# Routing rows in one piece: gate and token number inside the dispatched row, first group of the experts fixed and loaded one stage earlier, scatters of a group in parallel

## The chip, the core and the metric

One core of a Trainium2 chip. Five engines work side by side, each with its own instruction queue: TensorE (PE; its weight loads are listed as PEld), VectorE (DVE), ScalarE (ACT), GpSimd (POOL) and SyncE (SP), which here only issues DMAs. They are ordered by semaphores. DMAs are issued from the queues of SP and ACT, and from GpSimd where rows are addressed by an index held in memory (the indirect ones). The metric is the time of one execution on the device, in microseconds; the times before are the median of three runs.

## The reference, cut to what matters

A decoder of two layers on `x` of 32 x 128 tokens, 256 wide. The first five steps (two attentions and a quantised layer, then a gated attention with a long convolution, then a cross attention) are not touched by the change beyond what is told below. After each step comes `x = layernorm(x + step(x))`. The last step is a mixture of experts:

```python
logits = x_flat @ router_w.T                       # 4096 tokens, 8 experts
probs = softmax(logits); top_v, top_i = top_k(probs, 2); top_v /= sum(top_v)
for k in range(2):                                 # first and second choice
    pos = rank of the token within expert top_i[:, k]    # in token order
    keep = pos < C                                 # C = 1280 rows per expert and choice
    h = gelu(expert_in @ w1[expert])               # 256 -> 1024
    y = h @ w2[expert]                             # 1024 -> 256
    out += y[its row] * (top_v[:, k] * keep)
```

Each token is thus handled by two experts, and its two results, each times its gate, are added to it before the last layer norm.

## The kernel before

Seven stages run one after the other, each a block in which the five engines run their own programs. Between two stages stand a barrier, the clearing of semaphores by SyncE, and another barrier. Two stages matter, and one thing in the first.

**The first stage** (`l0_attn_heads`, L235). Beside its own work SyncE clears the DRAM table `xs` with zeros, in 32 pieces, one per tile of 128 tokens (`clear`, L373), and the small table `xm`. SyncE's queue issues in order: load an input tile, clear a piece, store a tile.

**The attention stage of the last layer** (`l1_xattn`, L1907). Tiles of 128 tokens, two tiles a group (`G = 2`), 16 groups, one walk step per tile; every engine has its list of work by lag behind the current tile `n`. Each tile has two halves `u` of eight heads:

- TensorE computes scores, VectorE takes maximum and difference (`shift`), ScalarE the exponential, VectorE sums and reciprocals (`sums`), GpSimd scales (`scale_e`, L2036), TensorE transposes (`transpose_e`, L2162), ScalarE copies, TensorE applies to the values, and the output projection follows two steps later (`multiply`, L2181).
- Four steps after its scores a group is normalised: VectorE gives mean and variance, GpSimd the root and shift (`roots`, L2042 to L2048), ScalarE writes the rows into `acc` (`normalise`, L2259), a tile buffer that holds all 32 tiles. SyncE stores them to the DRAM table `xo` (`store`, L2091).
- TensorE then transposes the rows and computes the router's logits; VectorE picks the two experts (`pick_expert`), TensorE counts ranks, VectorE turns them into a slot number per token and choice (`place_rows`, L2355 to L2373). ScalarE takes the exponential for the gate (`gate_exp`).
- Six steps behind, GpSimd dispatches a tile (`dispatch`, L2056 and L2058): for each of the two choices one indirect DMA writes the 128 rows into the table `xs` at their slots, and one writes gate and token number, two words a row, into the table `xm`. These are 4 DMAs a tile, 128 in all. GpSimd's order in an even step is: bias add for the group (`bias_x`), `scale_e` for both halves, dispatch; in an odd step: `scale_e` twice, `roots`, dispatch.
- After the last tile VectorE works out which expert and which place in `xs` each of 39 groups of 256 rows has (`map_groups`). The group with number 0 has a place that is known only then, like all others.

In `xs` each expert has a region of its own; slots that no token takes stay zero.

**The experts' stage** (`moe_experts`, L2413). For each of 39 groups `j`: SyncE loads 256 rows from `xs` (`load_x`, L2491), gates and numbers from `xm` (L2493) and the expert's 2 MB of weights (`load_w`, L2482; six buffers). TensorE runs `transposes(j)`, `up(j-1)` and `down_(j-2)` per step, 32 matmuls for each product; ScalarE applies the Gelu; VectorE multiplies the result with the gate (`gate_y`, L2585); GpSimd adds the rows to `xo` with an accumulating indirect DMA, one for each 128 rows (`add`, L2473). Each of these waits until the one before it has landed. Empty slots add to a spare tile behind the last token. When all have landed, SyncE reads the rows back (L2500), and VectorE and ScalarE do the last layer norm, whose results SyncE stores.

Of the kernel before, what the change touches and what calls it, by code (L numbers as in the profile page):

```python
# [116 lines left out]
def l0_attn(nc, x_in, wgv, bgv, wo, bo, x_out, xs, xm, xo, zero, zeroed, xo_stored):  # L117

    with ExitStack() as stack:
# [8 lines left out]
        l0_attn_heads(nc, x_in, gv, va, rn, lno, ln, ident, wo, bo, x_out, xs, xm, xo, zero, zeroed, xo_stored)  # L128
# [106 lines left out]
def l0_attn_heads(nc, x_in, gv, va, rn, lno, ln, ident, wo, bo, x_out, xs, xm, xo, zero, zeroed, xo_stored):  # L235
# [4 lines left out]
    with ExitStack() as stack:  # L240
# [54 lines left out]
        with nc.Block() as block:  # L295
# [54 lines left out]
            def _(sp):  # L350
# [16 lines left out]
                per_slot = xm.rearrange("(p n) d -> p (n d)", p=P)  # L367
                for i in range(META_PARTS):
                    part = per_slot[:, D * i:min(D * i + D, 2 * deep)]
                    sp.dma_start(part, zero[:, 0:part.shape[1]]).then_inc(zeroed, 16)  # L370
# [1539 lines left out]
def l1_xattn(nc, x_in, k_in, v_in, w, router, xs, xm, xs_zeroed, acc, meta, expert, place, dispatched, xo, xo_stored):  # L1910
# [3 lines left out]
    with ExitStack() as stack:  # L1914
# [38 lines left out]
        slot = kit.sb("slot", [P, TOPK, TILES], U32)  # L1953
        cnt, grp, end = (kit.sb(n, [P, EXPERTS]) for n in ("cnt", "grp", "end"))
# [13 lines left out]
                 "counted", "placed", "based", "mapped")  # L1968
# [5 lines left out]
         counted, placed, based, mapped) = (kit.sem(n) for n in names)  # L1974
# [22 lines left out]
        with nc.Block() as block:  # L1997
            @block.gpsimd
            def _(pool):
# [39 lines left out]
                def roots(g):  # L2039
                    item_done(pool, mv_done, g, G)  # L2040
                    slot_free(pool, normed, g, 2, G)
# [7 lines left out]

                def dispatch(n):  # L2050
                    g = n // G
                    item_done(pool, placed, g, PLACE_STEPS)
                    if n == 0:
                        pool.wait_ge(xs_zeroed, (ZERO_PARTS + META_PARTS) * 16)
# [678 lines left out]
```

## Time and profile before

| what | us |
|---|---|
| median of three runs (2752.1 to 2754.99) | 2754.79 |
| the profiled execution | 2750.7 |
| its span | 2749.0 |
| TensorE busy | 2367.3 (86%) |
| VectorE busy | 1401.6 (51%) |
| ScalarE busy | 1113.6 (41%) |
| GpSimd busy | 933.3 (34%) |
| DMA engines busy, queues of SP, of GpSimd, of ACT | 29.7%, 3.8%, 3.6% of 16 engines' span |

The shares are averages over seven stages with different limits; each stage has to be read by itself. The median of all runs is 4.1 us above the profiled one, and differences are worked out within the profiled execution. A busy share of a pipelined TensorE is not its share of peak.

How the rows further down are read: in a timeline a row has its start and its duration in us from the span's start, the engine, the line of the kernel, the operation, the tile written, the tile read, shapes, the count of merged instructions, and in brackets how long the engine had been idle before it and what ended the idle time. "issue" is idle time for which the profile shows no wait. SPq and POOLq are queues of an engine. The number behind a DMA issue is the median time from issue to landing.

### The profile page before, as it was taken

What the parts mean: (1) busy time and instruction counts of PE and PEld (TensorE: products, weight loads), DVE (VectorE), ACT (ScalarE), POOL (GpSimd) and SP (SyncE); (2) the same over time, 40 slices, a digit from 0 to 9 for tenths busy, and PEclk for the clock granted to TensorE, in tenths of its full rate; (3) what the DMA queues carried; (4) which work ended last, traced back from release to release, by engine and by line L of the source; (5) the groups of instructions that cost most, each with busy time, mean ns of one, the idle gap of its engine ahead of it and who ended that gap; (6) DMA issues with size and microseconds to landing.
All of it is one profiled execution on the core that took longest, in us unless ns stands there. A gap on an engine that the chain in (4) does not pass through costs nothing. (4 is left out here: it accounts for less than half of the span.)

```text
span 2749.0 us, 44609 instructions
## 1 busy us (share of the span) xinstructions
PE 2367.3 (86%) x17103; PEld 1815.4 (66%) x17134; DVE 1401.6 (51%) x2497; ACT 1113.6 (41%) x1898; POOL 933.3 (34%) x897
## 2 busy tenths in 40 slices
PE   9688887799995768978898869999995799999993
PEld 4466666466664546745665658887884688888883
DVE  5599898387775940003544536787776011111113
ACT  2466665356554644434333235555452111111113
POOL 2455554234443770000101024565556122222221
PEclk9799999899998889999999989999997899999997
DMA  2133324300101668552121033433431765666634
GB/s 73 53 103 117 116 98 146 108 16 24 47 16 58 211 173 205 160 182 93 31 62 46 16 133 99 106 97 97 117 88 43 291 188 180 177 184 190 191 85 134
DMA packets 227409, 313.11 MB, mean 114 GB/s; under 512 B 76672, under 2 KB 209792, under 8 KB 214016
## 3 DMA queue, kind: packets, MB, share of 16 engines
q1 hardware_dynamic: 201888, 253.82, 29.7%
q0 software_dynamic: 16352, 18.69, 3.8%
q10 hardware_dynamic: 8960, 37.75, 3.6%
q8 instruction: 138, 2.26, 0.3%
q14 instruction: 71, 0.58, 0.1%
HBM read 187.58 MB, written 122.63 MB: 113 GB/s over the span
## 5 line engine op out<-in xcount | busy, mean ns | idle before, releaser
L2548 ACT ACTIVATE me_h<-me_ps_h 128x512 f32<-128x512 f32 x156 | 93.1, 597 | 461.6 <-PE me_ps_h L2528 461.6
L2585 DVE TENSOR_SCALAR me_yo<-me_ps_y,me_mt 128x256 f32<-128x256 f32 x78 | 37.8, 484 | 473.6 <-PE me_ps_y L2537 454.8
L2528 PE MATMUL me_ps_h<-me_xt,me_w 128*128 128x256 f32 x1248 | 277.0, 380 | 0.0
L2537 PE MATMUL me_ps_y<-me_w,me_h 128*128 128x256 f32 x1248 | 275.6, 379 | 0.0
L2473 POOL DMA_INDIRECT xo<-me_yo,me_row x78 | 121.8, 1562 | 452.8 <-DVE me_yo L2585 306.9
L2537 PEld LDWEIGHTS me_ps_y<-me_w,me_h 128*128 128x128 f32 x1248 | 237.1, 190 | 32.2
L2528 PEld LDWEIGHTS me_ps_h<-me_xt,me_w 128*128 128x128 f32 x1248 | 235.1, 191 | 30.6
L327 POOL TENSOR_TENSOR l0ah_cm<-l0ah_c,l0ah_after 128x1024 f32<-128x1024 f32 x64 | 151.7, 2370 | 174.3 <-DVE l0ah_c L392 174.3
L666 POOL TENSOR_TENSOR l0x_en<-l0x_e,l0x_ri 128x1024 f32<-128x1024 f32 x64 | 120.0, 1896 | 210.7 <-DVE l0x_ri L888 210.7
L2036 POOL TENSOR_TENSOR l1x_e<-l1x_e,l1x_ri 128x1024 f32<-128x1024 f32 x64 | 121.8, 1902 | 195.6 <-DVE l1x_ri L2302 194.2
L987 PE MATMUL kv_ps<-kv_w_v,kv_ct 128*128 128x512 f32 x256 | 120.2, 609 | 24.7 <-PEq L82 15.3
L980 PE MATMUL kv_ps<-kv_ct,kv_w_k 128*128 128x256 f32 x512 | 121.3, 394 | 7.4 <-ACT kv_va L1026 4.9
L547 ACT ACTIVATE l0ah_f<-l0ah_ps_s 128x1024 f32<-128x1024 f32 x64 | 65.6, 1025 | 142.8 <-PE l0ah_ps_s L476 142.7
L2143 PE MATMUL l1x_ps_p<-l1x_xct,l1x_w_q 128*128 128x256 f32 x512 | 122.9, 384 | 0.0
L2181 PE MATMUL l1x_ps_o<-l1x_w_o,l1x_ot 128*128 128x256 f32 x512 | 118.7, 385 | 1.6 <-ACT l1x_ot L2254 1.6
L980 PEld LDWEIGHTS kv_ps<-kv_ct,kv_w_k 128*128 128x128 f32 x512 | 100.8, 199 | 28.7 <-ACT kv_va L1026 6.1
L2244 ACT ACTIVATE l1x_e<-l1x_sx 128x1024 f32<-128x1024 f32 x64 | 67.5, 1055 | 126.0 <-DVE l1x_sx L2293 126.0
L847 ACT ACTIVATE l0x_et<-l0x_ps_e 128x512 f32<-128x512 f32 x128 | 69.9, 595 | 100.5 <-PE l0x_ps_e L782 100.4
L1665 DVE TENSOR_SCALAR ma_zq<-ma_zp 128x1 f32<-128x1 f32 x1 | 0.2, 154 | 210.7 <-DMA ma_same<-in_msame 210.7
L1594 POOL TENSOR_TENSOR ma_ve<-ma_mv,ma_eps 128x4 f32<-128x4 f32 x8 | 2.9, 358 | 301.0 <-DVE ma_mv L1764 301.0
L2181 PEld LDWEIGHTS l1x_ps_o<-l1x_w_o,l1x_ot 128*128 128x128 f32 x512 | 94.7, 190 | 15.4 <-ACT l1x_ot L2254 1.9
L2299 DVE TENSOR_REDUCE l1x_rs<-l1x_e 128x8 f32<-128x1024 f32 x64 | 78.0, 1219 | 48.7 <-ACT l1x_e L2244 48.3
(381 smaller groups left out, 5303.0 us busy)
## 6 DMA issues: line engine op xcount, KB each, us to landing
me_w<-in_w SPq DMA_DIRECT2D x39, 2048.0 KB, 8.6
xs<-dec_zero SPq DMA_DIRECT2D x31, 1024.0 KB, 4.6
k<-kv_kt ACTq DMA_DIRECT2D x16, 1024.0 KB, 7.0
v<-kv_va ACTq DMA_DIRECT2D x16, 1024.0 KB, 6.1
l1x_kt<-k SPq DMA_DIRECT2D x16, 1024.0 KB, 7.3
l1x_va<-v SPq DMA_DIRECT2D x16, 1024.0 KB, 5.8
me_xg<-xs SPq DMA_DIRECT2D x39, 256.0 KB, 8.6
l0ap_x<-in_x SPq DMA_DIRECT2D x32, 128.0 KB, 2.0
```

Of the source, the lines that this page charges most:

```text
L327: pool.tensor_tensor(cm[:, n % 2, u, :, :], c[:, u, :, :], after[:, :].unsqueeze(1).to_broadcast([P, HALF, P]), ALU.add).then_inc(corr_mas ...
L666: pool.tensor_tensor(en[:, n % 2, u, :, :], e[:, n % 2, u, :, :], spread(ri[:, n % 2, u, :], P), ALU.mult).then_inc(e_scaled, 1)
L980: ins = pe.matmul(bank[:, c * self.GP:(c + 1) * self.GP], self.w_k[:, k, at], self.ct[:, g % 2, k, :], start=k == 0, stop=k == 1)
L987: ins = pe.matmul(bank[:, :], self.ct[:, g % 2, k, t * P:(t + 1) * P], self.w_v[:, k, 512 * c:512 * c + 512], start=k == 0, stop=k == 1)
L2036: pool.tensor_tensor(e[:, n % 2, u, :, :], e[:, n % 2, u, :, :], spread(ri[:, n % 2, u, :], P), ALU.mult).then_inc(e_scaled, 1)
L2143: last = pe.matmul(ps_p[i % 2][:, c * GP:(c + 1) * GP], w_q[:, k, at], xct[:, k, :], start=k == 0, stop=k == 1)
L2181: last = pe.matmul(ps_o[:, 0:2, :].rearrange("p a b -> p (a b)"), ot[:, c, :], w_o[:, c, :], start=c == 0, stop=c == C - 1)
L2299: dve.tensor_reduce(rs[:, n % 2, u, :], e[:, n % 2, u, :, :], AX.X, ALU.add).then_inc(summed, 1)
L2473: pool.indirect_dma_start(token_rows, bass.IndirectOffsetOnAxis(row[:, j % 2, q:q + 1], 0), yo[:, j % 2, q, :], None, compute_op=ALU.add). ...
L2528: last = pe.matmul(ps_h[i % HB][:, f % 2, :], w[:, j % WB, FFN * c + f * P:FFN * c + f * P + P], xt[:, j % 2, c, :], start=c == 0, stop=c ...
L2537: last = pe.matmul(ps_y[q][:, 0:D], h[:, j % 2, f, q * P:(q + 1) * P], w[:, j % WB, W2 + D * f:W2 + D * f + D], start=f == 0, stop=f == FC ...
L2548: act.activation(h[:, j % 2, 2 * i:2 * i + 2, :], ps_h[i % HB][:, :, :], ACT.Gelu).then_inc(gelued, 1)
```

## The change

- Table `xm` and tile `meta` are gone. A row of `xs` has 258 words instead of 256: the row, its gate, its token number plus one. In the attention stage a ring `row` of eight tiles (four groups) holds such rows for both choices. ScalarE writes every normalised row twice, once per choice (`normed`, `doubled`); GpSimd writes the numbers (`number_rows`), VectorE the gates. 64 indirect DMAs dispatch instead of 128. The ring's writers wait until the group four before has been dispatched and stored.
- The tile buffer `acc` is no longer needed by the attention stage and is allocated in the experts' stage.
- Every expert gets at least one group (first level -1 instead of 0), so group 0 is always the first of expert 0. Its weights are loaded in the attention stage after the last value tile, and its rows at that stage's end, when SyncE has waited for all dispatches. The experts' stage loads groups 1 to 38; one of the six weight buffers is the one filled early.
- In the experts' stage gates and numbers are read from the gathered rows, of which there are six buffers instead of four; a buffer is free when its group has been gated.
- The two accumulating DMAs of a group go out without waiting for each other; they wait for both of the group before. The spare rows are 256 instead of 128, so that no two of them meet.
- The clears of the first stage write rows of 258 words; two DMAs clear the spare rows of `xo`.

```diff
@@ l0_attn_heads
-                per_slot = xm.rearrange("(p n) d -> p (n d)", p=P)
-                for i in range(META_PARTS):
...
-                sp.dma_start(xo[TILES, :, :], zero[:, :]).then_inc(xo_stored, 16)
+                for i in range(GROUP // P):
+                    sp.dma_start(xo[TILES + i, :, :], zero[:, 0:D]).then_inc(zeroed, 16)
...
-                    sp.dma_start(part, zero[:, :].unsqueeze(1).to_broadcast([P, part.shape[1], D])).then_inc(zeroed, 16)
+                    sp.dma_start(part, zero[:, :].unsqueeze(1).to_broadcast([P, part.shape[1], ROW])).then_inc(zeroed, 16)
@@ l1_xattn
+        row = kit.sb("row", [P, ROW_SLOTS, TOPK, ROW])
+        number = kit.sb("number", [P, TILES])
+        dispatched = [kit.sem(f"dispatched{b}") for b in range(ROW_SLOTS // G)]
+        RG = ROW_SLOTS // G
...
-                pool.iota(meta[:, :, :, 1], pattern=[[0, TOPK], [P, TILES]], base=1, channel_multiplier=1,
+                pool.iota(number[:, :], pattern=[[P, TILES]], base=1, channel_multiplier=1,
...
+                pool.memset(levels[:, :, 0:1], -1.0).then_inc(cut, 1)
...
+                def number_rows(g):
+                    if g >= RG:
+                        pool.wait_ge(dispatched[g % RG], 16 * TOPK * G * (g // RG))
+                    at = G * g % ROW_SLOTS
+                    pool.tensor_copy(row[:, at:at + G, :, D + 1], number[:, G * g:G * g + G].unsqueeze(2).to_broadcast([P, G, TOPK])).then_inc(numbered, 1)
+
                 def dispatch(n):
                     g = n // G
                     item_done(pool, placed, g, PLACE_STEPS)
+                    item_done(pool, numbered, g)
+                    item_done(pool, doubled, g, G)
...
                     for k in range(TOPK):
                         pool.indirect_dma_start(xs, bass.IndirectOffsetOnAxis(slot[:, k, n:n + 1], 0),
-                                                acc[:, n, :], None).then_inc(dispatched, 16)
-                        pool.indirect_dma_start(xm, bass.IndirectOffsetOnAxis(slot[:, k, n:n + 1], 0),
-                                                meta[:, k, n, :], None).then_inc(dispatched, 16)
+                                                row[:, n % ROW_SLOTS, k, :], None).then_inc(dispatched[g % RG], 16)
...
-                     [(0, lambda n: scale_e(n, 0)), (0, lambda n: scale_e(n, 1)), (3, lambda n: roots(n // G)), (6, dispatch)])
+                     [(0, lambda n: scale_e(n, 0)), (0, lambda n: scale_e(n, 1)), (3, lambda n: roots(n // G)), (3, lambda n: number_rows(n // G)), (6, dispatch)])
...
+                    if g == NG:
+                        sp.dma_start(w_first[:, :], w12[0, :, :]).then_inc(w_loaded, 16)
                     if g >= 5:
                         store(g - 5)
+                for i in range(RG):
+                    sp.wait_ge(dispatched[i], 16 * TOPK * G * NG // RG)
+                sp.dma_start(xg[:, 0, :, :], xs[0:GROUP, :].rearrange("(q p) d -> p q d", p=P)).then_inc(xg_loaded, 16)
...
                 def normalise(g):
                     item_done(act, ln_done, g)
+                    if g >= RG:
+                        act.wait_ge(dispatched[g % RG], 16 * TOPK * G * (g // RG))
+                        act.wait_ge(xo_stored[g % RG], 16 * (g // RG))
                     for t in range(G):
-                        act.activation(acc[:, G * g + t, :], r[:, g % 2, t, :], ACT.Identity, scale=ln[:, g % 2, 0, t:t + 1],
+                        act.activation(row[:, (G * g + t) % ROW_SLOTS, 0, 0:D], r[:, g % 2, t, :], ACT.Identity, scale=ln[:, g % 2, 0, t:t + 1],
                                        bias=ln[:, g % 2, 1, t:t + 1]).then_inc(normed, 1)
+                    for t in range(G):
+                        act.activation(row[:, (G * g + t) % ROW_SLOTS, 1, 0:D], r[:, g % 2, t, :], ACT.Identity, scale=ln[:, g % 2, 0, t:t + 1],
+                                       bias=ln[:, g % 2, 1, t:t + 1]).then_inc(doubled, 1)
...
-                    then(dve.tensor_tensor(meta[:, :, n:n + G, 0], kept[:, :, :], gk[:, 3:5, :], ALU.mult))
+                    if rg >= RG:
+                        dve.wait_ge(dispatched[rg % RG], 16 * TOPK * G * (rg // RG))
+                    at = n % ROW_SLOTS
+                    then(dve.tensor_tensor(row[:, at:at + G, :, D].rearrange("p t k -> p k t"), kept[:, :, :], gk[:, 3:5, :], ALU.mult))
@@ moe_experts
+        def weights(j):
+            return w[:, j % WB - 1, :] if j % WB else w_first[:, :]
...
                 def add(j):
                     item_done(pool, row_ready, j)
+                    slot_free(pool, added, j, 1, 16 * Q)
                     for q in range(Q):
-                        n = Q * j + q
-                        item_done(pool, y_gated, n)
-                        slot_free(pool, added, n, 1, 16)
+                        item_done(pool, y_gated, Q * j + q)
...
                 def load_x(j):
-                    if j == 0:
-                        sp.wait_ge(dispatched, 16 * 2 * TOPK * TILES)
                     slot_free(sp, transposed, j, XB)
-                    slot_free(sp, y_gated, j, MB, Q)
-                    slot_free(sp, row_ready, j, MB)
+                    slot_free(sp, y_gated, j, XB, Q)
+                    slot_free(sp, row_ready, j, XB)
...
-                    sp.dma_start(mt[:, j % MB, :, :], blocks(xm)[bass.ds(b, 1), :, :, :].rearrange("b p q d -> (b p) q d")
-                                 ).then_inc(mt_loaded[j % MB], 16)
-
-                unrolled(GROUPS, [(0, load_x), (0, load_w)])
+                for j in range(1, GROUPS):
+                    load_x(j)
+                    load_w(j)
```

## Rows read from the trace of the kernel before

**Rows 1.** Busy time by stretches: start:end, length, then each engine's busy us (instructions).
```profile
1696.00:1725.00 29.00, 28.94 (x244) 24.49 (x243) 23.24 (x49) 15.90 (x29) 13.96 (x14) 1.00 0.44 101
...
2165.00:2705.00 540.00, 540.00 (x2574) 475.52 (x2573) 71.71 (x189) 89.55 (x150) 118.69 (x76) 1.00 0.57 172
```

**Rows 2.** Timeline, GpSimd, first operation of `roots`: start us, duration us, instruction.
```profile
1695.28 0.19 POOL L2042 TENSOR_TENSOR l1x_ln<-l1x_mv,l1x_eps 128x2 f32<-128x2 f32 x1
...
1724.51 0.19 POOL L2042 TENSOR_TENSOR l1x_ln<-l1x_mv,l1x_eps 128x2 f32<-128x2 f32 x1
...
2060.84 0.19 POOL L2042 TENSOR_TENSOR l1x_ln<-l1x_mv,l1x_eps 128x2 f32<-128x2 f32 x1
```

**Rows 3.** Timeline, attention stage: one group; last row from a later group.
```profile
1909.68 1.04 POOL L2056 DMA_INDIRECT xs<-moe_acc,l1x_slot  x1 [0.16 <-issue]
...
1913.61 0.20 DVE L2302 RECIPROCAL l1x_ri<-l1x_rs 128x8 f32<-128x8 f32 x1
...
1914.34 1.09 ACT L2259 ACTIVATE moe_acc<-l1x_r,l1x_ln 128x256 f32<-128x256 f32 x2
1914.55 1.27 POOL L2031 TENSOR_TENSOR l1x_xb<-l1x_x,l1x_b_all 128x512 f32<-128x512 f32 x1
...
1915.78 1.89 POOL L2036 TENSOR_TENSOR l1x_e<-l1x_e,l1x_ri 128x1024 f32<-128x1024 f32 x1
...
1916.27 1.06 ACT L2244 ACTIVATE l1x_e<-l1x_sx 128x1024 f32<-128x1024 f32 x1 [0.75 <-DVE l1x_sx L2293]
...
1917.73 1.09 PE L2162 MATMUL l1x_ps_e<-l1x_ident,l1x_e 128*128 128x128 f32 x8 [1.27 <-POOL l1x_e L2036]
...
1920.65 0.84 ACT L2237 ACTIVATE l1x_qt<-l1x_ps_p,l1x_b_q 128x256 f32<-128x256 f32 x2 [1.57 <-PE l1x_ps_p L2143]
...
2070.59 1.09 PE L2162 MATMUL l1x_ps_e<-l1x_ident,l1x_e 128*128 128x128 f32 x8 [3.20 <-POOL l1x_e L2036]
```

**Rows 4.** Timeline, end of the attention stage and start of the experts' stage.
```profile
2115.08 0.96 POOL L2058 DMA_INDIRECT xm<-moe_meta,l1x_slot  x1 [5.82 <-issue]
...
2115.88 0.17 DVE L2373 CAST l1x_slot<-l1x_sf 128x4 uint32<-128x4 f32 x1
...
2133.03 0.96 POOL L2058 DMA_INDIRECT xm<-moe_meta,l1x_slot  x1 [0.30 <-issue]
...
2138.36 0.20 POOL L111 MEMSET me_ident<- 128x128 f32 x1 [4.37 <-POOLq L82]
...
2141.15 0.35 SPq L2482 DMA_DIRECT2D me_w<-in_w  x1
...
2142.26 1.09 PE L2518 MATMUL me_ps_t<-me_ident,me_xg 128*128 128x128 f32 x4 [29.46 <-DMA me_xg<-xs]
...
2150.33 1.12 PE L2518 MATMUL me_ps_t<-me_ident,me_xg 128*128 128x128 f32 x4 [6.99 <-DMA me_xg<-xs]
...
2151.24 8.25 PE L2528 MATMUL me_ps_h<-me_xt,me_w 128*128 128x256 f32 x32
```

**Rows 5.** Timeline, end of the experts' loop.
```profile
2700.69 0.48 DVE L2585 TENSOR_SCALAR me_yo<-me_ps_y,me_mt 128x256 f32<-128x256 f32 x1 [2.90 <-PE me_ps_y L2537]
...
2702.96 1.56 POOL L2473 DMA_INDIRECT xo<-me_yo,me_row  x1 [2.88 <-DMA xo<-me_yo,me_row]
...
2707.59 0.48 DVE L2585 TENSOR_SCALAR me_yo<-me_ps_y,me_mt 128x256 f32<-128x256 f32 x1 [2.90 <-PE me_ps_y L2537]
...
2712.22 1.56 POOL L2473 DMA_INDIRECT xo<-me_yo,me_row  x1 [2.81 <-DMA xo<-me_yo,me_row]
...
2715.85 7.22 SPq L2500 DMA_DIRECT2D me_r<-xo  x8
```

**Rows 6.** DMA issues: count, KB, median us to landing; then starts of the clears.
```profile
xs<-dec_zero SPq DMA_DIRECT2D x31, 1024.0 KB, 4.6
...
xs<-moe_acc,l1x_slot POOLq DMA_INDIRECT x64, 4.6
...
L375 SPq DMA_DIRECT2D xs<-dec_zero x32: 425/436/1290, 83.6 to 471.7; - x32
```

More of the change, by code:

```diff
@@ L1907, in mega_attn, with l1_xattn @@
         kit.clear_semaphores()
-def l1_xattn(nc, x_in, k_in, v_in, w, router, xs, xm, xs_zeroed, acc, meta, expert, place, dispatched, xo, xo_stored):
+def l1_xattn(nc, x_in, k_in, v_in, w, router, w12, xs, xs_zeroed, w_first, xg, w_loaded, xg_loaded, expert, place, xo, xo_stored):
     G, W = 2, 64
@@ L1973, in l1_xattn @@
          r_loaded, preset, cut, y_transposed, xr_copied, routed, lg_copied, picked, gate_exped,
-         counted, placed, based, mapped) = (kit.sem(n) for n in names)
+         counted, placed, based, mapped, doubled, numbered) = (kit.sem(n) for n in names)
         x_loaded = [kit.sem(f"x_loaded{b}") for b in range(3)]
@@ L2090, in store @@
                     item_done(sp, normed, g, G)
-                    sp.dma_start(rows(xo, g), acc[:, G * g:G * g + G, :]).then_inc(xo_stored, 16)
+                    at = G * g % ROW_SLOTS
+                    sp.dma_start(rows(xo, g), row[:, at:at + G, 0, 0:D]).then_inc(xo_stored[g % RG], 16)
                 for g in range(2, NG + 5):
@@ L2191, in transpose_y @@
                         for k in range(2):
-                            last = pe.transpose(ps_p[1][:, (2 * t + k) * P:(2 * t + k + 1) * P], acc[:, G * rg + t, k * P:(k + 1) * P], ident[:, :])
+                            last = pe.transpose(ps_p[1][:, (2 * t + k) * P:(2 * t + k + 1) * P], row[:, (G * rg + t) % ROW_SLOTS, 0, k * P:(k + 1) * P], ident[:, :])
                     last.then_inc(y_transposed, 1)
@@ L2444, in moe_experts @@
          added, stats_done, mv_done, std_done, rstd_done, shift_done, normed, stored) = (kit.sem(n) for n in names)
-        w_loaded = [kit.sem(f"w_loaded{i}") for i in range(WB)]
-        xg_loaded = [kit.sem(f"xg_loaded{i}") for i in range(XB)]
-        mt_loaded = [kit.sem(f"mt_loaded{i}") for i in range(MB)]
+        w_loaded = [w_first_loaded] + [kit.sem(f"w_loaded{i}") for i in range(1, WB)]
+        xg_loaded = [xg_first_loaded] + [kit.sem(f"xg_loaded{i}") for i in range(1, XB)]
         r_loaded = [kit.sem(f"r_loaded{i}") for i in range(NB)]
+        def weights(j):
+            return w[:, j % WB - 1, :] if j % WB else w_first[:, :]
         def blocks(a):
@@ L2527, in up @@
                             for c in range(2):
-                                last = pe.matmul(ps_h[i % HB][:, f % 2, :], w[:, j % WB, FFN * c + f * P:FFN * c + f * P + P],
+                                last = pe.matmul(ps_h[i % HB][:, f % 2, :], weights(j)[:, FFN * c + f * P:FFN * c + f * P + P],
                                                  xt[:, j % 2, c, :], start=c == 0, stop=c == 1)
@@ L2537, in down_ @@
                             last = pe.matmul(ps_y[q][:, 0:D], h[:, j % 2, f, q * P:(q + 1) * P],
-                                             w[:, j % WB, W2 + D * f:W2 + D * f + D], start=f == 0, stop=f == FC - 1)
+                                             weights(j)[:, W2 + D * f:W2 + D * f + D], start=f == 0, stop=f == FC - 1)
                         last.then_inc(down, 1)
@@ L2676, in decoder_stages @@
     mega_attn(nc, x3, xn, mx, {k[1:]: v for k, v in t.items() if k[0] == "m"}, x4)
-    l1_tail(nc, x4, k1, v1, {k[1:]: v for k, v in t.items() if k[0] == "y"}, t["router"], t["w12"], xs, xm, xs_zeroed, xo, xo_stored, out)
+    l1_tail(nc, x4, k1, v1, {k[1:]: v for k, v in t.items() if k[0] == "y"}, t["router"], t["w12"], xs, xs_zeroed, xo, xo_stored, out)
 def kernel(**inputs):
```

70 lines of the change are left out of this document (35 added, 35 removed).

## The prediction

> **What bounds the kernel now.** I read the page's slices first, then the busy time by stretches, then the waits and the timeline of the two stages that the diff touches. The last layer's attention stage runs from 1589 to about 2138 us, the experts' stage from there to 2749. Nothing before 1589 is altered, but for the zeroing in the first stage.
>
> In the middle of the experts' stage TensorE has no gap: 540.00 us busy of 540 at full clock [rows 1]. The 2574 instructions there are 68 a group (4 transposes, 64 matmuls), so one group costs 540 / (2574 / 68) = 14.3 us; 39 groups come, and their number stays. Nothing that loads, gates or scatters during it can shorten it; gains lie at its two ends.
>
> In the attention stage TensorE is busy 28.94 us of 29 in the stretch 1696:1725 [rows 1], before GpSimd's scatters run in every step. `roots` comes once per group of two tiles, so its starts give the period: 29.23 us between 1695.28 and 1724.51, then 336.33 us over 11 groups, 30.57 each [rows 2]. So 1.34 us per group is lost once scatters run. The timeline of one group shows where: four scatters and the add of the bias stand on GpSimd between `roots` and the first `scale_e` of the next tile. VectorE has the reciprocal ready at 1913.81, GpSimd starts the scaling only at 1915.78, and TensorE's transposes of that tile wait 1.27 us for it [rows 3]. TensorE is the bound except for that wait, and the wait belongs to GpSimd's queue.
>
> **The change part by part.** All sums are against the profiled execution, 2750.7 us with a span of 2749.0; the median of the runs is 2754.79, 4.1 us (0.15%) higher, and I take differences over to it.
>
> *Half the scatters in the attention stage.* The gate and number ride in the row, so 64 of 128 scatters go. Four of them last from 1909.68 to 1914.55, 4.87 us, and with the gap between two each costs 1.27 us [rows 3]; two fewer are 2.5 us. One small copy of the token number is added behind `roots`; the nearest row is a GpSimd operation on 128x2 at 0.19 us [rows 2], and I take 0.25. The bias add then runs from about 1912.3 to 1913.6, and the scaling begins as VectorE's reciprocal ends, near 1913.9 instead of 1915.78. That is 1.9 us earlier, more than TensorE's 1.27, so the wait goes and 0.6 us of slack stays. A wider row might cost GpSimd more to issue. The dearest scatter in the trace is the accumulating one at 1.56 us against 1.04 [rows 3, 5]; with 0.5 to 0.6 more for each of the two, 1.1 us comes back and half the gain is left. I take 1.3 us x 11 groups = 14.3 us (bounds 0 and 14.7). The last group with projections over waits 3.20 us [rows 3]; of it I take 1.8 (0 to 2.3).
>
> *ScalarE writes every normalised row twice.* 32 activations more: 1.09 us a pair, 16 pairs, 17.4 us of engine time. Queued behind the second pair are the gate's exponential, the second exponential of the tile, and two bias passes of the projection. ScalarE stands idle 0.75 us before that exponential [rows 3], so it comes 0.3 us late. It then does 3.1 us of work and is free at about 1919.5, which is when TensorE, 1.27 us earlier than now, delivers the projection that is now biased at 1920.65. So the pair is just covered; without that cover it costs 1.09 us per group. In the drain of the stage, where projections have ended, one pair does lie ahead of the last output projection: -0.7 (0 to -1.1).
>
> *New waits in that stage.* ScalarE, VectorE and GpSimd now wait for a row buffer that was scattered and stored four groups before. Scatters of group g-4 are issued five tile steps, about 75 us, ahead of its reuse and land in 4.6 us [rows 6]. Cost nothing; what is queued behind the waiting instruction on each engine would be the exponentials, the placement and `scale_e`. Three new small operations in the setup have no reader for 100 us. Attention sum: 14.3 + 1.8 - 0.7 = 15.4 us.
>
> *The end of the stage.* The last slots are written at 2115.88, but GpSimd still has its backlog, with one stall of 5.82 us before 2115.08, and issues its last scatter at 2133.03; the next stage starts at 2138.36 [rows 4]. With half of them, tiles 28 and 29 are done before 2115.9, and the last four go out at 2116.3, 2117.6, 2118.9 and 2120.1. Here the change adds a wait: SyncE waits for all of them inside the stage, then issues the first gather. Landing takes 4.6 us [rows 6]: 2124.7, plus 0.5 for the issue. The way from there through the barrier is not shown alone; it is between 0 and the 4.37 us from GpSimd's last instruction to the next stage [rows 4]. I take 2.4, and 1 us for the chance that the stall moves along. Start at 2128.6 instead of 2138.4: 9.8 us (5.5 to 13).
>
> The Trainium skill (DMA: Bandwidth & Descriptors, "Anatomy of one DMA") gives about 2.0 us fixed cost for a GpSimd DMA, nearly all of it the receipt from memory. By it the landing would be 2.3 us and the gain 12.1; the trace shows 4.6, and I go by that.
>
> *First group loaded early.* Now the first gather lands by 2142.26, 3.9 us after the start. The 2 MB of weights go out at 2141.15, the second gather behind them, and TensorE gets its second transposes only at 2150.33 and the first up-projection at 2151.24, 12.88 us after the start [rows 4]. After: weights and first rows are there, the second gather stands first in the queue and lands 3.9 us after the start, and the up-projection follows 0.9 later, at 4.8. Gain 8.1 us (7 to 9). Next late are the second group's weights. They are issued about 2.3 us after the start and, like the first now, land within 9.2 (2141.15 to 2150.33), at 11.5; needed at 4.8 + 8.3 + 0.5 = 13.6. Two us of cover, none of it in the sum. The early weight load stands on SyncE behind the last value tile, when no input load is left; only stores of finished rows queue behind it.
>
> *In the middle of the experts' stage* 39 small loads go, and SyncE now waits for a gated group before it loads rows, ahead of the weights. Both are for six groups later, 85 us; nothing. The two extra words per row widen each gather by 0.8%.
>
> *Scatters in pairs.* Now each scatter waits for the one before it: 2702.96, 2712.22, rows read back at 2715.85 [rows 5]. After: the second of group 37 goes at 2701.9 (gated at 2700.69 + 0.48, plus 0.7 for the hand-over), lands 4.0 later at 2705.9; group 38's first starts 2706.6, its second needs its gated half (2707.59 + 0.48) and goes at 2708.8, landing by 2708.8 + 3.6 to 4.6. Readback at about 2712.9: 3.0 us (2 to 3.5). In the steady stretch GpSimd idles anyway.
>
> Sum: 15.4 + 9.8 + 8.1 + 3.0 = 36.3 us. 2754.8 - 36.3 = 2718.5 (the profiled one 2714.4).
>
> **The rivals.**
>
> *A. ScalarE takes GpSimd's place.* For it: the slack worked out above is nil, and the new pair is 1.09 us against a wait of 1.27. Against it: ScalarE is idle at other points of the group, and a delay of 0.2 or 0.3 leaves most of the gain. If the period stays at 30.57, 36.3 - 15.4 remains: 20.9, 2733.9 us. Half of it lost, as also with dearer wide scatters: 2726.
>
> *B. The boundary gives less:* the stall before 2115.08 falls behind the last slots in full and the barrier is the 4.37 us one. Start near 2133, gain 5.5 instead of 9.8: 2722.8. It speaks for it that the stall has a fetch's look, an engine waiting for nothing shown; against, that it took place once in 64 rounds.
>
> *C. Slower: zeroing.* 34560 rows are now cleared in pieces of 1032 bytes, at a pitch that is no multiple of 1024. A 1 MB clear lands in 4.6 us, and there is one per tile, 83.6 to 471.7, one in 12.5 us [rows 6]; each next input tile is loaded in the same queue behind it. From 12.5 us per clear the first stage waits for it; at 13.7 (three times now) 31 x 1.2 eats the whole gain, and at four times, 18.4 us, the loss is 31 x 5.9 = 183 - 36 = 147 us: 2901. Nothing in the trace asks for a factor of three. By the Trainium skill (same page, "How a descriptor splits into AXI transactions") a piece that starts off a 256-byte boundary takes one transaction or two more on top of four; that would be about 5.8 to 6.9 us, still covered. No row here shows an unaligned piece.
>
> *D. The change doesn't do what it says:* the early weights land late or the second weights bind (2 us of cover); gain of that part 4 instead of 8.1: 2722.6.
>
> **How the numbers follow.** Forecast 65%, A 14% (half of it at 2726, half at 2734), B and D together 15%, C 3%, something not named 3%, that I count half as no change, half as slower or little faster. What this kernel's measurement can tell from no change is 0.2%, 5.5 us; only C and part of the unnamed lie above 2749. Faster 0.94, same 0.02, slower 0.04. The range runs from all upper bounds that can meet (14.7 + 1.8 + 12 + 8.5 + 3.5 = 40.5, 2714, less 3 us for the spread of runs, 2711) to A in full, 2734.
>
> **What would show it.** Period of `roots` 29.2 to 29.4 us after scatters begin and no wait of TensorE for the scaled scores; if it is 30.6 with an idle TensorE that ScalarE releases, A. GpSimd's last attention scatter within 6 us of the last slots. First up-projection 4.8 us after the stage starts, 39 groups of 14.3 us. From last gated rows to readback about 4.9 us, now 7.8. Clears in the first stage landing under 7 us and that stage as long as now; if it is longer, C, and my forecast is wrong at its root.

## The result, and the profile after

| what | before, us | after, us |
|---|---|---|
| median of 4 runs each, same chip | 2753.44 (2749.68 to 2754.99) | 2714.71 (2710.74 to 2717.63) |
| the profiled execution, its span | 2750.7, 2749.0 | 2716.16, 2714.4 |
| ratio of the runs, 95% interval | | 0.9863 (0.9851 to 0.9875) |

The ratio is 37.7 us of 2753.4. Forecast were 36.3 us and 2718.5. Two further comparisons, each on its own chip, gave 0.9853 (0.9834 to 0.9872) and 0.9826 (0.9813 to 0.9839), which is 40.5 and 48.2 us between the medians. In the last the kernel before took 2760.83 us, 8 more than elsewhere, and the changed one 2712.65; why is open, since no profile of that slower one was taken. One execution of the changed kernel, the profiled one of the second comparison, ran slow (4140.42 us, mean granted clock 0.55): it is in no median, and its profile is not used.

Busy time by stretches after, columns as in [rows 1]. TensorE is as full as before in the steady part of either stage; in the second row 2575 instructions take 540 us, as 2574 did.

```profile
1699.00:1728.00 29.00, 28.95 (x245) 24.48 (x244) 23.21 (x50) 16.87 (x31) 12.30 (x12) 1.00 0.30 101
2131.00:2671.00 540.00, 540.00 (x2575) 475.49 (x2574) 68.55 (x188) 90.60 (x152) 117.52 (x76) 1.00 0.58 175
```

The timeline of GpSimd after: first operation of `roots`, for the groups that [rows 2] shows.

```profile
1698.57 0.19 POOL L2044 TENSOR_TENSOR l1x_ln<-l1x_mv,l1x_eps 128x2 f32<-128x2 f32 x1
...
1727.81 0.19 POOL L2044 TENSOR_TENSOR l1x_ln<-l1x_mv,l1x_eps 128x2 f32<-128x2 f32 x1
...
2049.42 0.19 POOL L2044 TENSOR_TENSOR l1x_ln<-l1x_mv,l1x_eps 128x2 f32<-128x2 f32 x1
```

Eleven groups now take 321.61 us, 29.24 each, where [rows 2] had 336.33: 14.7 us less. It is the period from before the first scatter: TensorE no longer waits for the scatters.

One group after, answering to [rows 3]: the copied number, two scatters where there were four, the scaling, the transposes, and ScalarE's doubled pair with what stands behind it.

```profile
1904.71 0.19 POOL L2056 COPY l1x_row<-l1x_number 128x4 f32<-128x4 f32 x1
...
1905.33 1.07 POOL L2066 DMA_INDIRECT xs<-l1x_row,l1x_slot  x1 [0.43 <-issue]
...
1906.70 0.96 POOL L2066 DMA_INDIRECT xs<-l1x_row,l1x_slot  x1 [0.31 <-issue]
...
1909.15 1.90 POOL L2038 TENSOR_TENSOR l1x_e<-l1x_e,l1x_ri 128x1024 f32<-128x1024 f32 x1 [0.17 <-DVE l1x_ri L2322]
...
1910.58 1.08 ACT L2279 ACTIVATE l1x_row<-l1x_r,l1x_ln 128x256 f32<-128x256 f32 x2
...
1911.65 1.09 PE L2176 MATMUL l1x_ps_e<-l1x_ident,l1x_e 128*128 128x128 f32 x8
...
1914.57 0.84 ACT L2251 ACTIVATE l1x_qt<-l1x_ps_p,l1x_b_q 128x256 f32<-128x256 f32 x2 [0.18 <-PE l1x_ps_p L2157]
```

The idle time at 1909.15 now ends with VectorE, so GpSimd is no longer late, and the transposes at 1911.65 name no releaser. ScalarE reaches the bias of the projection with 0.18 us to spare, where the prediction gave it none.

The end of the attention stage and the start of the experts' stage after, answering to [rows 4]:

```profile
2103.38 0.17 DVE L2396 CAST l1x_slot<-l1x_sf 128x4 uint32<-128x4 f32 x1
...
2103.82 0.96 POOL L2066 DMA_INDIRECT xs<-l1x_row,l1x_slot  x1 [3.40 <-DVE l1x_slot L2396]
...
2107.96 0.96 POOL L2066 DMA_INDIRECT xs<-l1x_row,l1x_slot  x1 [0.30 <-issue]
2110.88 0.37 SPq L2112 DMA_DIRECT2D moe_xg<-xs  x1
2114.97 0.20 POOL L111 MEMSET me_ident<- 128x128 f32 x1 [6.05 <-POOLq L82]
...
2117.20 0.35 SPq L2506 DMA_DIRECT2D me_w<-in_w  x1
...
2118.80 1.11 PE L2539 MATMUL me_ps_t<-me_ident,moe_xg 128*128 128x128 f32 x4 [2.01 <-DMA moe_xg<-xs]
...
2119.71 8.95 PE L2549 MATMUL me_ps_h<-me_xt,moe_w_first 128*128 128x256 f32 x32
```

GpSimd has no backlog left: at 2103.82 it waited 3.40 us for the last slots themselves. From the last slots to the next stage it is 11.6 us, before 22.5 [rows 4]. The first up-projection follows 4.7 us after the start, before 12.9.

The accumulating scatters at the end of the experts' loop and the readback, answering to [rows 5]:

```profile
2670.61 1.56 POOL L2497 DMA_INDIRECT xo<-me_yo,me_row  x1 [1.33 <-DVE me_yo L2607]
2675.01 1.56 POOL L2497 DMA_INDIRECT xo<-me_yo,me_row  x1 [2.85 <-DMA xo<-me_yo,me_row]
2677.51 1.56 POOL L2497 DMA_INDIRECT xo<-me_yo,me_row  x1 [0.94 <-DVE me_yo L2607]
...
2681.36 6.77 SPq L2521 DMA_DIRECT2D me_r<-xo  x8
```

And the DMA issues, answering to [rows 6]: the clears became slower, the scatters land sooner.

```profile
xs<-dec_zero SPq DMA_DIRECT2D x31, 1032.0 KB, 7.0
...
xs<-l1x_row,l1x_slot POOLq DMA_INDIRECT x64, 2.8
```

The whole way, cut at the same events in both traces (us):

| stretch | before | after | difference | forecast |
|---|---|---|---|---|
| to the start of the attention stage | 1588.98 | 1591.21 | +2.2 | 0 |
| its start to the first `roots` under scatters | 135.53 | 136.60 | +1.1 | 0 |
| 11 groups | 336.33 | 321.61 | -14.7 | -14.3 |
| last group | 28.94 | 25.92 | -3.0 | -1.8 |
| drain, to the last `roots` | 11.62 | 13.77 | +2.2 | +0.7 |
| last `roots` to next stage's start | 36.96 | 25.86 | -11.1 | -9.8 |
| start to first up-projection | 12.88 | 4.74 | -8.1 | -8.1 |
| to the readback | 564.61 | 561.65 | -3.0 | -3.0 |
| to the end | 33.15 | 33.04 | -0.1 | 0 |

They sum to -34.6, the difference of the spans. The first two lines move by themselves: over the twelve profiles used of all kernels here but the one with doubled zeroing, the stage started between 1586.6 and 1593.0, in no order by kernel, and the first `roots` of the stage came 77.2 to 79.0 us behind (77.3 before, 78.4 after).

### The profile page after: what moved, and what is told of

Its sections match the earlier page's. It is cut to its first block and busy times, and to the rows that moved or that the text cites. A ratio compares the mean times of both kernels' runs of the same rounds, so it can differ in the third digit from the quotient of the medians.

```text
span 2714.4 us, 44490 instructions
## 1 busy us (share of the span) xinstructions
PE 2370.4 (87%) x17103; PEld 1816.2 (67%) x17134; DVE 1388.5 (51%) x2497; ACT 1126.6 (42%) x1930; POOL 874.9 (32%) x850
## 2 busy tenths in 40 slices
DMA packets 214465, 313.23 MB, mean 115 GB/s; under 512 B 63856, under 2 KB 196848, under 8 KB 201072
## 5 line engine op out<-in xcount | busy, mean ns | idle before, releaser
L2607 DVE TENSOR_SCALAR me_yo<-me_ps_y,moe_xg 128x256 f32<-128x256 f32 x78 | 37.7, 484 | 476.3 <-PE me_ps_y L2558 410.0
L2549 PE MATMUL me_ps_h<-me_xt,me_w 128*128 128x256 f32 x1024 | 226.3, 379 | 0.0
L2558 PE MATMUL me_ps_y<-me_w,me_h 128*128 128x256 f32 x1024 | 226.1, 379 | 0.0
L2558 PEld LDWEIGHTS me_ps_y<-me_w,me_h 128*128 128x128 f32 x1024 | 194.6, 190 | 26.5
L2549 PEld LDWEIGHTS me_ps_h<-me_xt,me_w 128*128 128x128 f32 x1024 | 192.1, 190 | 24.8
L977 PEld LDWEIGHTS kv_ps<-kv_ct,kv_w_k 128*128 128x128 f32 x512 | 100.9, 199 | 30.5 <-ACT kv_va L1023 7.4
L2157 PEld LDWEIGHTS l1x_ps_p<-l1x_xct,l1x_w_q 128*128 128x128 f32 x512 | 93.5, 192 | 12.6 <-ACT l1x_xct L2243 0.3
```

What stands on the lines that cost most here:

```text
L977: ins = pe.matmul(bank[:, c * self.GP:(c + 1) * self.GP], self.w_k[:, k, at], self.ct[:, g % 2, k, :], start=k == 0, stop=k == 1)
L2157: last = pe.matmul(ps_p[i % 2][:, c * GP:(c + 1) * GP], w_q[:, k, at], xct[:, k, :], start=k == 0, stop=k == 1)
L2549: last = pe.matmul(ps_h[i % HB][:, f % 2, :], weights(j)[:, FFN * c + f * P:FFN * c + f * P + P], xt[:, j % 2, c, :], start=c == 0, stop=c ...
L2558: last = pe.matmul(ps_y[q][:, 0:D], h[:, j % 2, f, q * P:(q + 1) * P], weights(j)[:, W2 + D * f:W2 + D * f + D], start=f == 0, stop=f == F ...
```

## The experiments

**Scatters in series again.**

```diff
-                    slot_free(pool, added, j, 1, 16 * Q)
                     for q in range(Q):
+                        slot_free(pool, added, Q * j + q, 1, 16)
```

> The changed kernel, with the accumulating scatters of the experts' stage one behind the other again: each waits for the one before it, not only each group for the group before it. Theory: the pairs are worth the 3.0 us by which the way from the first up-projection to the readback of the rows became shorter; that way goes back from 561.7 to about 564.6 us and the whole from 2714.7 to 2717.7, while stage starts stay. Rival: the 3 us came from somewhere else in the stage (no small loads in front of the weights); then that way stays at 561.7.

2719.54 us median against 2714.71; first up-projection to readback 565.4 against 561.65 us: 3.8 more. The last scatters and the readback:

```profile
2677.20 1.56 POOL L2497 DMA_INDIRECT xo<-me_yo,me_row  x1 [2.96 <-DMA xo<-me_yo,me_row]
2681.69 1.56 POOL L2497 DMA_INDIRECT xo<-me_yo,me_row  x1 [2.93 <-DMA xo<-me_yo,me_row]
...
2685.29 6.77 SPq L2521 DMA_DIRECT2D me_r<-xo  x8
```

4.5 us from one to the next, each released by the DMA of the one before it. The theory holds, at a little over the 3.0 us expected, and the rival is out. The 3.0 us were themselves a net figure: the first up-projection, which lies in the same stretch, took 8.95 us in the changed kernel and 8.25 before [rows 4], so the pairs are worth about 3.7.

**First group loaded late.** The loads of group 0 go back from the attention stage to the head of the experts' loop.

```diff
-                        sp.dma_start(w_first[:, :], w12[0, :, :]).then_inc(w_loaded, 16)
-                sp.dma_start(xg[:, 0, :, :], xs[0:GROUP, :]...).then_inc(xg_loaded, 16)
-                for j in range(1, GROUPS):
+                for j in range(GROUPS):
```

> The changed kernel, with the rows and weights of group 0 loaded at the start of the experts' stage instead of in the attention stage; the wait for all dispatches stays where it is. Theory: the first up-projection goes from 4.7 us after the stage's start back to 12.3 to 12.9, and the whole becomes 7.5 to 8.1 us slower (2722.5). The stage itself starts earlier by no more than the 0.1 us of an issue. Rival: the attention stage ends 2 to 4 us earlier because nothing is loaded at its end, and the net loss is 4 to 6 us.

2721.89 us median, 7.2 more. TensorE at the start of the stage, which is at 2112.62:

```profile
2123.61 1.11 PE L2536 MATMUL me_ps_t<-me_ident,moe_xg 128*128 128x128 f32 x4 [6.07 <-DMA moe_xg<-xs]
2124.51 9.05 PE L2546 MATMUL me_ps_h<-me_xt,moe_w_first 128*128 128x256 f32 x32
```

11.9 us after the start, 7.15 later than with the early load. That is a little under the 7.5 to 8.1 expected; that the small loads of gates, in this queue before the change, are gone here too would fit it. From the last scatter's issue to the stage's start it is 7.01 us, as with the early gather, so the early gather costs the boundary nothing. The rival is out.

**The small scatters back.** Beside each row scatter one of two words per row, into a table that nobody reads.

```diff
+                        pool.indirect_dma_start(xm, bass.IndirectOffsetOnAxis(slot[:, k, n:n + 1], 0),
+                                                row[:, n % ROW_SLOTS, k, D:D + 2], None)...
```

> The changed kernel, with one more scatter of two words per row for each of the 64 row scatters in the attention stage, into a table that nothing reads, as GpSimd had it before; everything else stays as changed (ScalarE still writes each row twice). Theory (GpSimd's queue set the period): from the first scatters on a group takes 30.5 us again instead of 29.24, TensorE waits again 1.3 us a group for the scaled scores (GpSimd), the last group gives back about 3 us and the stage's end 8 to 11; the whole is 26 to 29 us slower, about 2742. Rival (the period fell because VectorE and SyncE have fewer things to wait for, or because rows are no longer accumulated in one large buffer): the period stays near 29.3 and only the end of the stage is late, 8 to 11 us, about 2725.

2744.85 us median, 30.1 more: most of the gain is gone. The period is 31.02 us in ten of eleven groups and 33.03 in one, where 30.5 was expected. The waits of TensorE between 1720 and 2070: their whole time, how often, the longest.

```profile
PE l1x_ps_e L2179 <- POOL l1x_e L2039: 19.2, 11, 2.0
```

The rows of the kernel before and of the changed one, for 1720 to 2060, are

```profile
PE l1x_ps_e L2162 <- POOL l1x_e L2036: 13.9, 11, 1.3
```

```profile
PE l1x_ps_e L2176 <- POOL l1x_e L2038: 1.3, 1, 1.3
```

The small scatters on GpSimd are the cause; nothing else of the change went back. The period is 0.45 us above the one before. The new copy of 0.19 us and the idle 0.43 us ahead of the first scatter (0.16 in [rows 3]) would make 0.46. The backlog at the end is back too: the last scatter goes out 12.6 us after the last slots, and the next stage starts 19.2 us after them (11.6 in the changed kernel, 22.5 before). From the last scatter to that start it is 6.6 us here.

**One copy.** ScalarE writes each row once, and both scatters send it (the second choice goes out with the first one's gate).

```diff
-                                                row[:, n % ROW_SLOTS, k, :], None)...
+                                                row[:, n % ROW_SLOTS, 0, :], None)...
-                        act.activation(row[:, (G * g + t) % ROW_SLOTS, 1, 0:D], r[:, g % 2, t, :], ...)
```

> The changed kernel, with ScalarE writing each normalised row once and both scatters of a tile sending that one copy (so the second choice goes out with the first one's gate: its output is not the reference's). It measures what the second copy costs. Theory: in the steady part of the attention stage it is covered, the period stays at 29.24 us (within 0.1); in the drain one pair less lies ahead of the last output projection and 0.6 to 1.1 us are saved there; the whole is 0.6 to 1.5 us faster (2713.6). Rival (ScalarE is now as near to the bound as GpSimd): the period falls further, to 29.1 or less, and 2 to 3 us more are won over 11 groups.

2714.29 us median against 2714.71. The period is 29.24 us again: the second copy is covered in the steady part. In the drain, where projections have ended, TensorE waits 0.69 us for ScalarE's copy `xr` of the transposed rows instead of 1.32, so a pair costs 0.6 us there. The rival is out.

**TensorE's order at the start**, run in two comparisons.

```diff
-                unrolled(GROUPS, [(0, transposes), (1, up), (2, down_)])
+                transposes(0)
+                up(0)
+                transposes(1)
+                for j in range(2, GROUPS + 2): ...
```

> The changed kernel, with TensorE doing the up-projection of group 0 before the transposes of group 1, whose rows are still on their way. Theory (the first up-projection waits only behind those transposes): it starts 1.6 to 1.8 us after the stage's start instead of 4.7, but the second one then needs the second group's weights at about 11 us and these land at 11 to 11.5, so 2.0 us stay of the 3.1 (2.0 to 3.1; 2712.7). Rival: the second group's weights land only after 13 us; then nothing is left of it.

> The changed kernel unaltered, beside the three that build on it. Both theories: 2713 to 2717 us. Its profile tells whether the slower last output projection of the drain (5.39 us against 3.70) belongs to the kernel (then it is 5.39 again) or to the one execution (then it is 3.70 and the drain is 1.7 us shorter).

> The kernel with group 0's up-projection ahead of group 1's transposes once more. Theory: 1.4 us faster than the changed kernel, as the way from the stage's start to the readback was (564.99 against 566.39 us); over all runs of both the medians differ by 0.5 to 2.5. Rival: the difference was the clock's phase, and it is within 0.5 or of the other sign.

> The changed kernel unaltered once more, for a profile at full clock and as the partner of the kernel with group 0's up-projection first. 2711 to 2716 us. If the last output projection of the drain is 3.70 us here, the drain is 12.0 us from the roots of tiles 28 and 29 to those of the last two, against 11.6 before, 0.4 to 0.7 more.

Medians: 2710.22 against 2712.06 in the first comparison, 2712.27 against 2712.65 in the second; over all runs compared 2711.99 (9) against 2712.46 (14). The first up-projection of the two executions of this one kernel:

```profile
2111.43 8.55 PE L2549 MATMUL me_ps_h<-me_xt,moe_w_first 128*128 128x256 f32 x32 [0.95 <-DVE me_xt L2599]
```

```profile
2114.22 10.07 PE L2549 MATMUL me_ps_h<-me_xt,moe_w_first 128*128 128x256 f32 x32 [0.95 <-DVE me_xt L2599]
```

Either starts 2.8 us after its stage, 2 us sooner than in the changed kernel (4.7, 4.8). That is later than the 1.6 to 1.8 expected: VectorE's copy of the transposes, hidden before behind the second ones, is now waited for. From the stage's start to the readback the two need 564.99 and 566.51 us, the changed kernel 566.39 and 566.43. The same 32 matmuls took 8.55 or 10.07 us, at a mean granted clock of 0.83 and 0.71. So an earlier start of 2 us is worth anything from 1.4 us to nothing, and between the kernels no difference is shown: neither the 2.0 us expected first nor the 1.4 expected then came, and 0.4 in the second comparison is what the rival there allowed. On the drain, the unaltered kernel's profile of the second comparison has 5.39 us for its last output projection again. But the two executions of the kernel with this new order have 3.70 and 5.39, so it does not belong to a kernel.

**TensorE kept busy.** The same kernel, with matmuls at the end of the attention stage.

```diff
+                item_done(pe, based, NG - 1)
+                for i in range(16):
+                    pe.matmul(ps_p[0][:, :], ones[:, :], w_q[:, 0, 0:2 * GP], start=True, stop=True)
```

> The same, and TensorE does 16 matmuls of 128 x 512 that nobody reads after its last work in the attention stage, so that it is less long idle before the experts' stage. Theory (the granted clock after the boundary depends on how long TensorE was idle): the first up-projection takes 8.25 us instead of 8.95 and more, up to 1.9 us beyond the kernel without them. Rival: TensorE is idle again for 8 us or so before the stage anyhow, the clock is the same and nothing is won, or the extra matmuls end late and cost up to 1 us.

2714.67 us median, 4.5 more than without them. The timeline of TensorE:

```profile
2099.07 16.75 PE L2239 MATMUL l1x_ps_p<-l1x_w_q,l1x_ones 128*128 128x512 f32 x32 [0.77 <-DVE l1x_pos L2380]
2117.28 0.66 PE L2542 MATMUL me_ps_t<-me_ident,moe_xg 128*128 128x128 f32 x4 [1.46 <-POOL me_ident L113]
2118.89 8.53 PE L2552 MATMUL me_ps_h<-me_xt,moe_w_first 128*128 128x256 f32 x32 [0.95 <-DVE me_xt L2602]
```

They took 16.75 us at a mean granted clock of 0.83 and ended 9.8 us after the last scatter went out, so the stage began 10.6 us after it instead of 7.0. TensorE was then idle for 1.46 us only, not 15.4, and the up-projection still took 8.53 us, at a granted clock of 0.84. The theory is not borne out: without the long idle time ahead of it this up-projection is as slow as in the better of the two executions above. It is one execution, and what makes it slow is open.

**Rows of 1280 bytes.**

```diff
-ROW = D + 2
+ROW = D + 64
```

> The changed kernel with rows of 320 words (1280 bytes, a multiple of 256) instead of 258; the 62 added words are written as zero. All clears, scatters and gathers move a quarter more. It tests why the clears of the first stage took 7.0 us where they took 4.6 with rows of 256 words. Theory (rows that start at no multiple of 256 bytes): 1280 bytes start on one again, a clear moves 1.24 times as much and lands in 5.2 to 5.8 us in spite of it. Rival (any pitch other than 1024, or simply more bytes): 7.0 to 8.7 us. Time of the whole: the same within 2 us, since the clears are hidden either way; gathers of 320 kB take 0.3 to 0.5 us longer at the start of the experts' stage.

2712.97 us against 2712.06. The clears of this kernel:

```profile
xs<-dec_zero SPq DMA_DIRECT2D x31, 1280.0 KB, 5.2
```

1280 kB land in 5.2 us, 1032 kB in 7.0. More bytes in less time, in as many packets (214465 in either profile): the count of bytes doesn't make the clears slow, and neither does just any pitch other than 1024. With 1032 bytes both the start and the end of a row lie off a multiple of 256, so which of the two costs the time is not shown. Gathers of 320 kB take 3.1 us against 2.8.

**GpSimd's relief alone.** The kernel before, without its small scatters.

```diff
-                        pool.indirect_dma_start(xm, bass.IndirectOffsetOnAxis(slot[:, k, n:n + 1], 0),
-                                                meta[:, k, n, :], None).then_inc(dispatched, 16)
```

> The kernel before without its 64 scatters of gate and number (that table stays zero, so every routed row goes to the spare tile with gate 0: the routed experts' part is left out of the output). Nothing else of the change: no second copy by ScalarE, no wider row, no early first group, adds in series. It measures the relief of GpSimd alone. Theory: period from 30.57 to 29.24 us (14.7 over 11 groups), the last group 3 more, the stage ends some 10 us earlier behind its last slots: 26 to 29 us faster, about 2725. Rival (the end of the stage gained because of the new wait and the early gather): 17 to 19 us, about 2735.

2722.94 us. In this comparison the kernel before took 2760.83, so the ratio (0.9865) would say 37; against the 2753 of the other three comparisons it is 30. The profile decides by stretches: attention stage 522.3 us against 549.38 before and 523.76 changed, period 29.24. The wait of TensorE for GpSimd is gone in all groups but one (1720 to 2060):

```profile
PE l1x_ps_e L2160 <- POOL l1x_e L2036: 1.3, 1, 1.3
```

Its boundary, from the last slots on:

```profile
2097.38 0.17 DVE L2371 CAST l1x_slot<-l1x_sf 128x4 uint32<-128x4 f32 x1
...
2101.96 0.96 POOL L2056 DMA_INDIRECT xs<-moe_acc,l1x_slot  x1 [0.30 <-issue]
2108.91 0.20 POOL L111 MEMSET me_ident<- 128x128 f32 x1 [5.99 <-POOLq L82]
```

11.5 us, and 6.95 from the last scatter to the start, with no wait of SyncE for it and no gather in the stage. All of the attention stage's gain is GpSimd's relief, and beside this kernel the new wait costs nothing. The rival is out. Where GpSimd has its backlog the space is not 7.0 us: 5.3 in the kernel before, without the wait, and 6.6 with the small scatters back, with it. What sets it in either case is open.

**Zeroing doubled.** A second table of the same size is cleared, one more 1 MB piece per tile.

```diff
+                    sp.dma_start(part2, zero[:, :].unsqueeze(1).to_broadcast([P, part.shape[1], ROW])).then_inc(zeroed, 16)
```

> The changed kernel that clears, besides the dispatch table, a second table of the same size that nobody reads, one more piece of 1 MB per tile in the first stage, in the same queue. It tries the price of the rival that the zeroing becomes the bound: two pieces of 7.0 us per tile are 14 us, against a tile each 12.5 us. Theory (the queue is a line, and a clear blocks it until it has landed): the first stage becomes 31 x 1.5 = 47 us longer and the whole about 2760. Rival (the input tiles are loaded two ahead and a clear only shares the 16 engines with them): the stage stays as long within 5 us and the last pieces, of 2.8 MB, push the time by 0 to 10.

2747.17 us, 32 to 35 more than the changed kernel. Both pieces of this kernel, DMA issues:

```profile
xs_twice<-dec_zero SPq DMA_DIRECT2D x31, 1032.0 KB, 7.4
xs<-dec_zero SPq DMA_DIRECT2D x31, 1032.0 KB, 11.2
```

The stage is 32.4 us longer. The next-to-last clear is issued 19.7 us later (490.69 against 471.00), 0.64 per tile, and the pieces at the end, 2.8 MB each, hold the queue for the rest. Neither number was met. The two pieces overlap and land in about 11.7 us, not 14, yet the tile is lengthened already there, before the 12.5 us that the prediction named. The load and the store of the tile stand in the same queue and may be why; no run tries it.

## Why the prediction was right

The forecast of 2718.5 us missed by 3.8, a tenth of the gain, of which 1.4 is that the median before came out lower this time. Within the profiled executions the gain is 34.6 where 36.3 was forecast. That nearness is in part luck: the stretches that the change does not touch moved 3.3 us the wrong way, and the others gave 37.9. The mechanisms, though, came as told, and most of them have an experiment of their own.

*GpSimd's queue sets the wait.* Forecast 14.3, measured 14.7; with the small scatters back the wait of TensorE returns, and when they alone leave the kernel before it goes. The whole 1.34 us per group came back, so the 0.6 us of slack computed for GpSimd was enough.

*The last group* gave 3.0, above the range's 2.3. The step took only 1.8 of a wait of 3.20 us; 0.46 is left of it, and the output projection waits 0.2 less for ScalarE. The term was cautious without a reason from the rows.

*ScalarE's second copy* costs nothing in the steady part, and rival A with it; the one-copy kernel shows it. In the drain it costs 0.6, forecast 0.7. But that line of the table came to 2.2, outside the 0 to 1.1 given for it, and the other 1.7 us are clock: the last 16 output matmuls took 5.39 us instead of 3.70. Two kernels with the same drain, the changed one and the one with the first group late, in the timeline of TensorE:

```profile
2082.44 5.39 PE L2195 MATMUL l1x_ps_o<-l1x_w_o,l1x_ot 128*128 128x256 f32 x16
```

```profile
2081.32 3.70 PE L2192 MATMUL l1x_ps_o<-l1x_w_o,l1x_ot 128*128 128x256 f32 x16
```

The mean granted clock over them was 0.68 and 1.00, so part of the first ran at the lower level (1.2 of 2.4 GHz). Seven of the nine profiles with the second copy and without small scatters have the slow one (5.35 or 5.39); the three without a second copy (before, one copy, relief alone) have 3.70. TensorE's idle time ahead of it is longer with the second copy, 1.32 us against 0.69 to 0.74. But that alone does not bring the fall: three profiles have 1.32 or 1.33 us and 3.70 nevertheless (late first group, small scatters back, one of the two with the up-projection first). Its cause is open. The prediction priced instructions and not the clock.

*The boundary* gave 10.9 behind the last slots, forecast 9.8; the sum was right and its parts were not. The landing took 2.9 us from the last scatter's start, not the median of 4.6 [rows 6]; that median had come from the small scatters between (5.0 when they are back, 2.8 without). The way through the barrier was 4.1 and not 2.4. And the kernel without the wait shows that the sum's chain is not what holds the stage back: 7.0 us pass from the last scatter either way. The stall of 5.82 us [rows 4] did not fall behind the last slots, so rival B is out. It did not come back at all: in none of the other profiles used does GpSimd stand idle over 1.5 us ahead of a scatter of this stage with no releaser named, not even with the small scatters back. So up to 5.8 of the 10.9 us may be that stall, which one profile shows, and not the number of scatters; only more profiles of the kernel before could tell. The Trainium skill (DMA: Bandwidth & Descriptors, "Anatomy of one DMA") gives about 2.0 us of fixed cost; here the trace, with 2.9, is nearer to that than to the median that I went by.

*The early first group* gave 8.1, as forecast, and the kernel without it loses 7.2. Rival D is out: the second up-projection begins at 2128.93, right behind the transposes ahead of it, so the second weights were in time.

*Pairs of scatters* gave 3.0 net, as forecast, and 3.8 by the experiment.

*Zeroing* stayed hidden at 7.0 us a clear, at the limit that I gave: the stage behind it starts at 501.42 us, before at 500.97. Rival C's mechanism is real, but its price was wrong: at 11.7 us of clears per tile the stage has already grown, and where between 7.0 and 11.7 it begins is not shown. The Trainium skill (same page, "How a descriptor splits into AXI transactions") gives more transactions to a piece that starts off a 256-byte boundary. The trace agrees that such rows are dearer, but not with the count: by the Trainium skill's rule a piece of 1032 bytes at these starts (multiples of 8) works out to five transactions, not up to the six that the prediction allowed, and an aligned one of 1280 bytes to five as well. Yet 1032 kB took 7.0 us, just above the 5.8 to 6.9 of the prediction, and 1280 kB took 5.2.

The gain splits so: some 27 us from GpSimd's relief (14.7 in the groups, 3 in the last, 10.9 at the end with the stall in it, less the drain), 7 to 8 from the early group, 3 to 4 from the pairs.

## What to carry to other kernels

An indirect scatter of 128 rows costs its engine the same whatever the rows' length: 0.96 us busy in most rows, with 8 bytes a row, with 1032 and with 1280. Two words that travel in a row already sent cost GpSimd one copy of 0.19 us a group here; sent by themselves they cost 1.27 us a scatter, in the middle and again as backlog at the end. A resource that waits 1.3 us in each group is best found by the period of one operation, before and after the suspected work begins. At the head of a stage list what the first matmul waits for, and load it in the stage before, where its landing is hidden behind the barrier. And take the landing of one late DMA from a single row of the timeline, not from a median over a crowded stage.

## What the runs showed of the hardware

- A DMA that writes rows of 1032 bytes at that pitch takes 7.0 us for 1 MB, with 1024-byte rows 4.6, with 1280-byte rows 5.2 for 1.25 MB.
- Scatters by GpSimd land in 2.8 us in the median where half as many are issued (4.6 before, 5.0 with the small ones back).
- Between GpSimd's last scatter and the next stage lie 7.0 us, whether another queue waits for its landing (7.01) or not (6.95); behind a backlog of scatters it was 5.3 and 6.6.
- The granted clock after a boundary differs between executions of one kernel: 0.83 and 0.71 over the same 32 matmuls. Matmuls that fill the idle time ahead of them did not raise it beyond that (0.84).
- The last 16 output matmuls of the attention stage took 3.70 us in one execution of the kernel with the up-projection first and 5.39 in the other, at granted clocks of 1.00 and 0.68.
